# Normalising the last layer's tokens by halves: squares, sums, factors and chunks of one half before those of the other

## The reference, cut to what matters

```
def rmsnorm(x, w):
    v = jnp.mean(jnp.square(x), axis=-1, keepdims=True)
    return x * jax.lax.rsqrt(v + EPS) * w
h = rmsnorm(x, ln1_w)                    # the first normalisation
q, k, v = h @ wq, h @ wk, h @ wv         # 16 heads of 128
x = x + softmax_causal(q k / sqrt(128)) v @ wo
t = rmsnorm(x, ln2_w)                    # the second normalisation
logits = t @ gate_w.T                    # 16 experts, top 6 by softmax
out = x + routed experts(t) + shared expert(t)
```

## Time and profile before

| what | value |
|---|---|
| median of 3 runs | 964.62 us (962.67 to 965.97) |
| profiled execution, its own time | 965.51 us |
| its span, first to last instruction | 963.8 us |
| mean granted TensorE clock | 0.899 of full speed |
| PE busy | 793.4 us, 82% of the span |
| DVE / ACT / POOL busy | 583.7 / 372.3 / 228.3 us |
| first normalisation (before attention) | 381.5 to 399.0 us of the span |
| second normalisation (before the experts) | 712.9 to 730.3 us |
| attention / experts | 399.0 to 711.9 / 730.3 to the end |

### The profile page before, as it was taken

The page is one execution under the profiler, slowest core; times in us unless marked ns, Lnnn a source line. Parts: engine busy times, 40 slices in busy tenths (PEclk is TensorE's granted clock), DMA queues, the critical chain, the costliest instruction groups (busy, mean ns, idle before and its releaser), DMA issues. The chain is left out here.

```text
span 963.8 us, 11159 instructions
## 1 busy us (share of the span) xinstructions
PE 793.4 (82%) x3628; PEld 592.3 (61%) x3633; DVE 583.7 (61%) x1267; ACT 372.3 (39%) x820; POOL 228.3 (24%) x215
## 2 busy tenths in 40 slices
PE   0776679778885545899999999999978999999995
PEld 0332346534443124788788877887867788888884
DVE  6889599879997894365656555655534333323333
ACT  2400411225423654364454544544443333334331
POOL 0400000150131430221020110210010554555452
PEclk9888788689895877699999999999986999999997
DMA  4000000753311001210110101000020523133421
GB/s 139 0 2 0 1 0 1 274 217 98 99 48 46 1 0 34 98 45 1 45 42 3 44 1 45 1 1 1 1 68 3 132 66 99 55 88 91 91 46 44
DMA packets 37374, 49.85 MB, mean 52 GB/s; under 512 B 18670, under 2 KB 30038, under 8 KB 35654
## 3 DMA queue, kind: packets, MB, share of 16 engines
q1 hardware_dynamic: 36262, 46.90, 15.8%
q0 software_dynamic: 768, 2.10, 0.7%
q10 hardware_dynamic: 288, 0.14, 0.1%
HBM read 43.00 MB, written 6.13 MB: 51 GB/s over the span
## 5 line engine op out<-in xcount | busy, mean ns | idle before, releaser
L2120 DVE TENSOR_TENSOR B_l<-bank,TW_l 128x512 f32<-128x512 f32 (+1 forms) x50 | 34.6, 692 | 140.7 <-PE bank L2065 140.7
L1739 ACT ACTIVATE EX<-EX,nm 128x128 f32<-128x128 f32 (+1 forms) x128 | 57.5, 450 | 108.3 <-DVE nm L1788 107.8
L1689 POOL TENSOR_TENSOR WL<-RAW,WH 128x512 fp32r<-128x512 f32 x32 | 41.1, 1290 | 232.5 <-ACT WH L1713 232.5
L2155 POOL TENSOR_TENSOR HL_l<-H_l,HH_l 128x512 fp32r<-128x512 f32 (+1 forms) x50 | 64.1, 1283 | 119.6 <-ACT HH_l L2134 119.6
L2065 PE MATMUL bank<-XH,WH_l 128*128 128x512 f32 (+1 forms) x200 | 80.0, 400 | 0.0
L2065 PE MATMUL bank<-XL,WH_l 128*128 128x512 f32 (+1 forms) x200 | 79.7, 399 | 0.0
L2065 PE MATMUL bank<-XH,WL_l 128*128 128x512 f32 (+1 forms) x200 | 79.5, 398 | 0.0
L1802 DVE TENSOR_TENSOR AL<-bank,AH 128x256 fp32r<-128x256 f32 x64 | 27.2, 424 | 62.2 <-ACT AH L1754 62.2
L1842 PE MATMUL bank<-XH,WH 128*128 128x512 f32 x128 | 59.7, 466 | 3.9 <-DVE XL L1545 3.9
L134 POOL TENSOR_TENSOR WV<-EUK,V 128x512 f32<-128x512 f32 x16 | 23.1, 1450 | 167.0 <-DVE GAIN L219 166.9
L2142 ACT ACTIVATE S_l<-bank 128x512 f32<-128x512 f32 (+1 forms) x50 | 30.1, 602 | 84.0 <-PE bank L2065 84.0
(11 more groups left out here) (303 smaller groups left out, 2100.8 us busy)
## 6 DMA issues: line engine op xcount, KB each, us to landing
RAW<-l_attn SPq DMA_DIRECT2D x8, 1024.0 KB, 4.8
WE<-l_experts SPq DMA_DIRECT2D x1, 6144.0 KB, 22.6
RAW_l<-l_experts SPq DMA_DIRECT2D x9, 512.0 KB, 4.0
TW_l<-routed SPq DMA_DIRECT2D x16, 256.0 KB, 5.2
RAW<-l_w SPq DMA_DIRECT2D x3, 1024.0 KB
TW_l<-routed SPq DMA_DIRECT2D x14, 192.0 KB, 3.2
RAW_l<-l_experts SPq DMA_DIRECT2D x9, 256.0 KB, 4.6
sorted_x<-ZERO SPq DMA_DIRECT2D x1, 1920.0 KB, 8.1
```

The source lines that it names most:

```text
L1689: pool.tensor_tensor(WL[:, slot, c], RAW[:, slot, c], WH[:, slot, c].bitcast(F32), ALU.subtract).then_inc(w_low, 1)
L1739: act.activation(EX[:, s, a:b], EX[:, s, a:b], ACT.Exp, bias=nm[:, s, i:i + 1], scale=scale, accum_out=rs[:, s, i:i + 1]).then_inc(expd, 1)
L2120: v.tensor_tensor(self.B[0:rows, q % 2], self.k.banks[2 * (q % 2) + 1][0:rows], self.TW[0:rows, w % self.TWS, n * W:(n + 1) * W], ALU.mult ...
L2155: pool.tensor_tensor(self.HL[0:rows, q % 4], self.H[0:rows, q % 2], self.HH[0:rows, q % 4].bitcast(F32), ALU.subtract).then_inc(self.h_low, 1)
```

## The change

Each normalisation is cut by token halves. ScalarE squares four chunks of 512 in `ORDER` instead of two of 1024. TensorE waits for two of them, sums the first 512 tokens into bank 0, then the second 512 into bank 3, and signals each half; the spreading matmuls wait for each half's factors. VectorE and ScalarE make mean, root and reciprocal for tokens 0 to 511 (`factors(0)`), then for the rest (`factors(1)`), as two instructions of 4 columns in place of one of 8. The chunks then go in pairs: HN, HN, XL, XL of the first half, then of the second. On TensorE the projection's n = 0 waits for two XL, n = 1 for four; the router waits for two ahead of its first 128 tokens and for four ahead of token 512.

```
     def squares(self, act, k):
-        for h in range(KD):
-            act.activation(self.SQ[:, h], k.XC[:, h], ACT.Square).then_inc(self.sq, 1)
+        for j in ORDER:
+            act.activation(chunk(self.SQ[:], j), chunk(k.XC[:], j), ACT.Square).then_inc(self.sq, 1)
 
     def scalar(self, act, k):
-        act.wait_ge(self.mean, 1)
-        act.activation(self.rt[:], self.ms[:], ACT.Sqrt).then_inc(self.root, 1)
-        for n in range(NCH):
-            act.wait_ge(self.xn, n + 1)
-            j = ORDER[n]
+        for n in range(2):
+            t = slice(4 * n, 4 * n + 4)
+            act.wait_ge(self.mean, n + 1)
+            act.activation(self.rt[:, t], self.ms[:, t], ACT.Sqrt).then_inc(self.root, 1)
+        for i, j in enumerate(ORDER):
+            act.wait_ge(self.xn, i + 1)
             act.activation(chunk(self.XH[:], j), chunk(self.HN[:], j), ACT.Copy).then_inc(self.xh, 1)
 
     def vector(self, v, k, LN):
...
+        def factors(n):
+            t = slice(4 * n, 4 * n + 4)
+            v.wait_ge(self.sums, n + 1)
+            v.tensor_scalar(self.ms[:, t], k.banks[3 * n][:, 0:4], 1.0 / D, EPS3, ALU.mult, ALU.add).then_inc(self.mean, 1)
+            v.wait_ge(self.root, n + 1)
+            v.reciprocal(self.rstd[:, t], self.rt[:, t]).then_inc(self.rec, 1)
...
+        factors(0)
+        factors(1)
+        normalised(0)
+        normalised(1)
+        self.low(v, 0)
+        self.low(v, 1)
+        normalised(2)
+        normalised(3)
+        self.low(v, 2)
+        self.low(v, 3)
 
     def tensor(self, pe, k):
...
+        for n in range(2):
+            pe.wait_ge(self.sq, 2 * n + 2)
+            for t in range(4):
+                at = (4 * n + t) * P
+                for h in range(KD):
+                    mm = pe.matmul(k.banks[3 * n][:, t:t + 1], self.SQ[:, h, at:at + P], k.ONES[:, 0:1],
+                                   start=(h == 0), stop=(h == KD - 1))
+            mm.then_inc(self.sums, 1)
+        for n in range(2):
+            pe.wait_ge(self.rec, n + 1)
...
@@ project, in attention
                 if n == 0:
                     pe.wait_ge(w_low, 4 * (g + 1))
-                    if not later(g):
-                        pe.wait_ge(norm.xl, NCH)
+                if not later(g) and n < 2:
+                    pe.wait_ge(norm.xl, 2 * (n + 1))
@@ the router, in the experts
-            pe.wait_ge(norm.xl, NCH)
             pe.wait_ge(r_in, 16)
             for t in range(NT):
+                if t % 4 == 0:
+                    pe.wait_ge(norm.xl, 2 * (t // 4 + 1))
```

More of the change, by code:

```diff
@@ L1525, in scalar @@
+        for i, j in enumerate(ORDER):
+            act.wait_ge(self.xn, i + 1)
             act.activation(chunk(self.XH[:], j), chunk(self.HN[:], j), ACT.Copy).then_inc(self.xh, 1)
     def vector(self, v, k, LN):
[L1528 to L1535, removed]
-            v.scalar_tensor_tensor(chunk(self.HN[:], j), chunk(k.XC[:], j), LN[:, self.col, j // 2:j // 2 + 1],
-                                   k.banks[1 + n // 2][:], ALU.mult, ALU.mult).then_inc(self.xn, 1)
-            if n >= 1:
-                self.low(v, n - 1)
@@ L1540, in vector, with normalised @@
-        self.low(v, NCH - 1)
+        def factors(n):
[4 more added lines that the diff above has]
+            v.reciprocal(self.rstd[:, t], self.rt[:, t]).then_inc(self.rec, 1)
+        def normalised(i):
+            j = ORDER[i]
+            v.wait_ge(self.spread, i // 2 + 1)
+            v.scalar_tensor_tensor(chunk(self.HN[:], j), chunk(k.XC[:], j), LN[:, self.col, j // 2:j // 2 + 1],
+                                   k.banks[1 + i // 2][:], ALU.mult, ALU.mult).then_inc(self.xn, 1)
@@ L1548, in tensor @@
     def tensor(self, pe, k):
[L1550 to L1562, removed]
+        for n in range(2):
[8 more added lines that the diff above has]
+            pe.wait_ge(self.rec, n + 1)
+            for t in range(4):
+                mm = pe.matmul(k.banks[1 + n][:, t * P:(t + 1) * P],
+                               self.rstd[:, 4 * n + t:4 * n + t + 1].to_broadcast([P, P]), k.IDF[:], start=True, stop=True)
+            mm.then_inc(self.spread, 1)
 def each_group(eng, body):
```

## The result

The changed kernel takes 955.66 us (median of 6 runs, 954.61 to 956.91) against 964.46 us of the kernel before (6 runs). The ratio is 0.9904 with a 95% interval of 0.9889 to 0.9918: 8.8 us by the medians, 7.9 to 10.7 by the interval. The forecast was 958.4 us, range 956.0 to 961.4.

What follows compares the result with a forecast made beforehand. PE, busy 82% of the span, was taken as the bound. Savings of 3.0 + 3.9 = 6.9 us gave 958.6 from the profiled 965.51; less 0.5, 958.2 from the median. Forecast 958.4 us, range 956.0 to 961.4.

Steps and rivals of the forecast that it cites:

- Squares, sums, factors: Both normalisations: sums begin 0.85 us earlier, table load then ends last, spreading starts 0.54 and 1.25 us earlier.
- Chunks and waits: XL pairs let the projection's n = 1 start 3.0 us earlier and the router 3.9 us earlier.
- The rival of the held-back factors: Second half's factors on DVE, ahead of the first HN, hold the first half back; 959.2 us, chance 0.04.
- that of the fixed wait in attention: Attention's first group waits for something with a fixed time, absorbing the 3.0 us; 961.5 us, chance 0.08.
- what is late next is the clock: First normalisation: behind the projection's waiting n = 1, ACT and DVE are not late; the clock is, at no gain.
- the clock is earlier: Rise up to 3 us sooner in the first stage, 1.5 us more saved; 956.9 us, chance 0.10.
- the gap sets the clock back: New 0.16 us gap in the projection delays the clock's rise, 1.3 to 2 us lost; 960.0 us, chance 0.15.
- The clock in the second normalisation: Clock may hold into the second sums in the median run, so 0.5 us is taken off the saving.
- Attention and experts as long as before: Attention and experts were to take the same time as before, a difference of 0.
- a wait of more than 2 us: Slower rival: only such a PE wait in attention drops the clock enough; 967.5 us, chance 0.03.

Runs made afterwards that it cites:

- one_wait: The changed kernel, but the projection's n = 0 waits for all four XL again; 958.58 us, ratio 0.9933.
- before_prefill: The kernel before with 2 idle matmuls between sums and spreading of both normalisations; 962.77 us, one run.
- after_again: The changed kernel run once more, nothing altered, to see where its clock changes stand; 956.65 us, one run.
- before: The kernel before, unchanged; 964.46 us median of 6 runs, its profiled execution 965.51 us.
- before_again: The kernel before run once more, nothing altered, to see where its clock changes stand; 964.99 us, one run.
- before_tail: The kernel before with 8 idle matmuls in PE's wait ahead of the last 12 down matmuls; 962.37 us, ratio 0.9983.
- before_fill: The kernel before with 9 idle matmuls in PE's wait between spreading and projection of the first normalisation; 961.25 us, ratio 0.9962.
- a_only: The kernel before with halves in the first normalisation and the projection's waits only; 957.25 us, ratio 0.9926.
- after: The changed kernel in its first profile; profiled execution 955.24 us, median of 6 runs 955.66 us.
- after_tail: The changed kernel with 8 idle matmuls ahead of the last 12 down matmuls; 955.04 us, ratio 0.9890.

## Why the prediction was right, and where it was not

**Squares, sums, factors.** Right. Four squares took 2.19 us (2.20 forecast), the sums began 1.20 us behind them (1.21), and the table load took the sums' place: the spreading began at 391.57 - 382.22 = 9.35 us (9.32), and in the second at 8.40 (8.60). The drain of about 1380 ns that the Trainium skill states ("ScalarE: Activation LUTs", section "What ACT_TABLE_LOAD costs") does not show here: the root follows the load by 0.01 and 0.02 us.

**Chunks and waits.** Right. n = 0 at 14.40 us behind the squares (14.37), n = 1 at 17.02 (17.08), the router at 13.45 (13.55), no wait in its middle. The wait between n = 0 and n = 1 was to be under 0.3 us and was 0.99: n = 0 ran at full clock and was through sooner, while n = 1 waits for the last XL whatever PE does. The rival of the held-back factors and that of the fixed wait in attention are out: the longest PE wait there is still 1.0 us for PN, and attention took 305.6 us.

**The clock behind the first normalisation.** This is the step that failed. I wrote "what is late next is the clock" and then counted its rise from the projection's first matmul, 5.1 us as before, at no gain. It rose 1.8 us ahead of that matmul instead. In four of the five profiles of the kernels in the table above with halves there it rose before the projection (in one_wait only to fall again); in the changed kernel that was worth 1.0 us, 4.30 instead of 5.28 us from n = 1 to the scores; what n = 0 gained by it was lost in the wait of 0.99 us. The rival "the clock is earlier" had the right sign, a chance of 0.10 and the wrong ground: one_wait shows that the rise does not need the shorter gap behind the spreading, and in before_prefill's one profile starting PE's work earlier ahead of it was enough. The rival "the gap sets the clock back" is out: gaps of 1.47 and 0.99 us left it at full, and in after_again, which had the small gap, it rose 4.4 us behind the projection's first matmul.

**The clock in the second normalisation.** This failed in size. Of the 0.9 us between the profiled execution and the median before, I took 0.5 us off the saving, for executions in which the clock holds longer and the sums are sooner done. No profile of the kernel before shows that: in before, before_again, before_tail and before_fill the spreading began 9.83 to 9.85 us behind the second squares. Only a_only's does (8.97). So up to 0.5 of the 2.6 us that the forecast lacks is this term; without it the sum from the median would have given 957.7 instead of 958.2. What I left out is a gain: the router, begun 4 us earlier and more, met a stretch of full clock in six of eight profiles, worth 0.8 us.

**"Attention and experts as long as before".** This failed too, and in this pair of profiles it is the larger part, 2.2 us. I never looked at the experts' end. There PE waits 2.15 us, and the clock had fallen behind it. My own condition for a fall was "a wait of more than 2 us", and I asked it of attention alone. before_tail shows what such a fall costs the kernel before, 1.6 to 2.2 us; how much of it the change itself frees, and how much was the luck of one execution, stays open.

**The sum.** Chain 3.2 + 4.0 = 7.2, clock behind the first normalisation 1.0, end 2.2: 10.4 us; the table's small differences take 0.1 off, which makes the 10.3 us between the two spans. The median difference, 8.8 us, is less, since the clock's terms are not the same in every execution. From the squares on, after_again took 573.8 us: of its 8.5 us under before, the chain is 2.7 + 4.1, the clock 0.3 behind the first normalisation, 0.8 in the router and 0.8 at the end, and small differences take 0.1 off. The two profiles of each kernel, 582.3 and 581.4 against 571.3 and 573.8, differ by 9.3 us in the mean. The range, 956.0, left these terms out: it took the clock's bounds for the two stretches that the change touches and for no other, though the three known runs already spread over 3.3 us. The chances have a slip as well: those on the side of "faster" add up to 0.93, not 0.91.

**Still open.** What sets the clock's changes apart between executions of one kernel (after and after_again; 4.76 and 4.17 us at the end in two profiles of before), by how much the changed kernel's end is better on average, and how often its router meets the full clock.

## What to carry to other kernels

When PE's waits are shortened, price the clock over the whole kernel: list every wait of PE of about 2 us and more, near the change or not, with the granted clock behind it, and let the range hold what each could give or take. Here the clock stayed up behind waits of 1.47 and 1.53 us, and the shortest behind which it fell at once was one of 2.15. A wait that is free in the chain may still cost its successor half its speed; a few idle matmuls in it show in one run what it is worth (2.3 us, and 1.6 to 2.2 us here). Compare two profiles from a point up to which they run the same instructions, since what lies ahead of it scattered by 5 us. And after a chain is shortened, look at what ends last now: here a table load that one instruction could move. It brought 3.3 us more, of which the chain accounts for 2.2 in the profile.

## What the runs showed of the hardware

- The clock's changes mostly kept their distance to the program. In 11 of 14 profiles the fall came 1.0 to 1.3 us ahead of the first squares and in the other three 4.4 us; the rise stood 12.4 to 12.7 us behind them in seven profiles and 22.6 to 22.8 in four, with 16.0, 16.1 and 19.2 us in the last three.
- Two savings in one kernel need not add up: 7.7 and 6.1 us alone, 8.8 together. In the profiles most of the difference is what the clock gave at three places.
- Idle bf16 matmuls of 512 columns kept the clock at full through a 2.15 us wait (before_tail, after_tail). In the 3.9 us wait of before_fill it rose at 398.0, 2.2 us after they began, and not in the projection.
- In the changed kernel's profile the granted clock stayed at half through 7 us of sum matmuls (383.4 to 390.4) and rose during the spreading behind them (394.8).
- A table load was followed at once by its user: the root began 0.01 and 0.02 us behind the load's end (391.10 and 717.03).
